# A gated cross-attention kernel on one core: the order of its first stage rewritten, with the next batch's correlation products placed right behind the picking and the context transformed two batches ahead

## What is computed

```python
x = x + tanh(g_xattn[0]) * autocorrelation(layernorm(x), ctx, ctx)
x = x + tanh(g_ffn[0])   * routed_lora_ffn(layernorm(x))
x = x + tanh(g_xattn[1]) * cross_attention(layernorm(x), ctx)
x = x + tanh(g_ffn[1])   * lora_ffn(layernorm(x))
```

```python
corr = ifft(fft(q) * conj(fft(k))).real        # per channel, over 128 lags
w, idx = top_k(corr, 9)                        # 9 = int(2 * ln 128)
w = softmax(w)
out = sum_i w_i * v[min(idx_i + pos, L - 1)]
```

## Time and profile before

| | us |
|---|---|
| median of 3 runs (815.9 to 818.12) | 816.29 |
| the profiled execution | 813.65 |
| its span in the trace | 811.9 |
| PE busy | 774.1 (95%) |
| DVE busy | 577.2 (71%) |
| ACT busy | 412.1 (51%) |
| POOL busy | 364.9 (45%) |

### The profile page before, as it was taken

One profiled execution on the slowest core, in us unless ns is written; L12 is line 12 of the kernel. 1 busy time (PEld: TensorE's weight loads), 2 busy tenths in 40 slices (PEclk: granted clock), 3 DMA queues, 4 the chain that ended last, 5 costly groups with the idle time before them and its releaser, 6 DMA issues.

```text
span 811.9 us, 13195 instructions
## 1 busy us (share of the span) xinstructions
PE 774.1 (95%) x4224; PEld 631.9 (78%) x4224; DVE 577.2 (71%) x1283; ACT 412.1 (51%) x1142; POOL 364.9 (45%) x420
## 2 busy tenths in 40 slices
PE   4699999988999999999999999999999999999998
PEld 1355554667888888888888888888888888888776
DVE  3689999756767777676777766677776666677774
ACT  3246664456545555554565546445555545454521
POOL 1356776646334533643353246424533643254532
PEclk9899999999999999999999999999999999999999
DMA  7300003103100300120031003000310101000002
GB/s 284 115 27 27 26 27 98 45 1 103 29 1 1 105 27 2 42 76 14 1 92 27 14 1 105 27 2 1 104 28 1 52 28 53 1 14 1 1 28 77
DMA packets 16979, 34.61 MB, mean 43 GB/s; under 512 B 2320, under 2 KB 2448, under 8 KB 16656
## 3 DMA queue, kind: packets, MB, share of 16 engines
q1 hardware_dynamic: 16912, 33.78, 13.1%
HBM read 31.67 MB, written 2.10 MB: 42 GB/s over the span
## 4 chain that ended last, share of the span: by engine, by line
PE 68%; DVE 17%; POOL 7%; issue 6%; ACT 1%; DMA 1%; SPq 0%; POOLq 0%; DVEq 0%; ACTq 0%
PE pair L825 17%; PE pair L826 17%; PE pair L827 17%; PE pair L924 4%; PE pair L937 3%; PE pair L986 3%; POOL qkr L512 2%; POOL probn L504 2%; PE pair L926 1%; DVE prod L1160 1%; DVE wlag L1186 1%; POOL wo_lo L498 1%; DVE xres L1243 1%; DVE score L1260 1%; DVE rest L1170 1%
## 5 line engine op out<-in xcount | busy, mean ns | idle before, releaser
L504 POOL TENSOR_TENSOR probn<-prob,erec 128x512 f32<-128x512 f32 x64 | 66.9, 1046 | 162.2 <-DVE erec L1275 162.2
L1299 DVE TENSOR_TENSOR qkn<-pair,qkr 128x640 f32<-128x640 f32 x64 | 52.8, 825 | 91.0 <-POOL qkr L512 91.0
L1280 DVE TENSOR_REDUCE qkss<-qksq 128x5 f32<-128x640 f32 x64 | 52.6, 822 | 86.4 <-ACT qksq L698 86.4
L691 ACT ACTIVATE prob<-score,nmax 128x128 f32<-128x128 f32 x256 | 99.6, 393 | 20.4 <-DVE nmax L1262 18.7
L680 ACT ACTIVATE oT_hi<-pair 128x512 fp32r<-128x512 f32 x64 | 38.2, 597 | 136.2 <-PE pair L827 136.2
L825 PE MATMUL pair<-wq_hi,nT_hi 128*128 128x512 f32 x256 | 105.8, 413 | 0.0
L825 PE MATMUL pair<-wo_hi,oT_hi 128*128 128x512 f32 x256 | 100.8, 394 | 2.8 <-issue 2.8
L827 PE MATMUL pair<-wq_hi,nT_lo 128*128 128x512 f32 x256 | 100.4, 392 | 0.0
L826 PE MATMUL pair<-wo_lo,oT_hi 128*128 128x512 f32 x256 | 100.2, 392 | 0.0
L826 PE MATMUL pair<-wq_lo,nT_hi 128*128 128x512 f32 x256 | 100.2, 391 | 0.0
L827 PE MATMUL pair<-wo_hi,oT_lo 128*128 128x512 f32 x256 | 99.6, 389 | 0.0
(11 more groups left out here) (174 smaller groups left out, 1995.9 us busy)
## 6 DMA issues: line engine op xcount, KB each, us to landing
wq_raw<-in_wq SPq DMA_DIRECT2D x32, 256.0 KB, 2.8
wo_raw<-in_wo SPq DMA_DIRECT2D x32, 256.0 KB, 2.9
wkv_raw<-in_wkv SPq DMA_DIRECT2D x8, 512.0 KB, 4.8
ctxn<-in_ctx_n SPq DMA_DIRECT2D x8, 256.0 KB, 2.9
ctxt<-in_ctx_t SPq DMA_DIRECT2D x8, 256.0 KB, 2.6
out<-wkv_raw SPq DMA_DIRECT2D x8, 256.0 KB, 2.0
xres<-in_x SPq DMA_DIRECT2D x1, 1280.0 KB, 11.7
wbase<-in_wbase SPq DMA_DIRECT2D x1, 1024.0 KB, 9.0
```

Source lines behind the costliest of these rows:

```text
L504: pool.tensor_tensor(probn[:], prob[:], erec[:].unsqueeze(2).broadcast_to([P, HG, P]), ALU.mult).then_inc(normed, 1)
L691: t = act.activation(prob[:, h, :], score[:, h, :], ACT.Exp, bias=nmax[:, h:h + 1], accum_out=esum[:, h:h + 1])
L1280: dve.tensor_reduce(qkss[:], qksq[:], AX.X, ALU.add).then_inc(qk_ss, 1)
L1299: dve.tensor_tensor(qkn[:], qk_bank, qkr[:].unsqueeze(2).broadcast_to([P, HG + 1, P]), ALU.mult).then_inc(qk_nat, 1)
```

## The change

Nothing is computed differently; apart from one subtraction cut in two and one transfer cut in two, the instructions are the same and stand in another order.

- **DVE:** `corr_product(b+1)` comes right behind `pick_lags(b)` and no longer behind `out_products(b)`. The statistics of batch b+2 come behind `out_products(b)` (from b = 2 on) and are woven into `route(b-1)`.
- **PE:** the context transforms of slot b are those of batch b+2. `q_transform(b+1)` stands in the middle of `base_products(b-2)`, `turn_lags(b)` before `routed_product(b-2)`, `correlation(b+1)` before the last two context transforms, and parts of `project_kv(0)` and `project_q(0)` move from the tail into slot 6.
- **ACT:** the normalisation of batch b+1 (`nx`) stands at the start of slot b, ahead of `high_turned_ctx(b)` and the exponentials; the copies of the context are those of b+2 and come after the normalisations; the weights are split one slot earlier.
- **POOL:** `add_bias(b-2)` moves behind `lag_weights(b)`, `sums(b)` before `f_scale(b+2)`, the weights' low parts move one slot earlier (slots 3, 4 and 5 in place of 4, 5 and 6), and `low_wkv` is two operations of 128x512 in place of one of 128x1024.
- **SP:** `dft` comes in two pieces, the first three matrices ahead of the first context; the gates come later. In the tail `squares`, `high_v`, `inverse_norms`, `copy_rows` and their like change places with neighbours.

```diff
                 load_batches(0)
+                sp.dma_start(dft[:, 0:V_IM + 1, :], dft_d[:, 0:V_IM + 1, :]).then_inc(ld_dft[0], 16)
                 load_ctx(0)
-                sp.dma_start(dft[:], dft_d[:]).then_inc(ld_dft, 16)
-                sp.dma_start(gates_in[:], gates[:]).then_inc(ld_g, 16)
+                sp.dma_start(dft[:, V_IM + 1:N_DFT, :], dft_d[:, V_IM + 1:N_DFT, :]).then_inc(ld_dft[1], 16)
                 load_batches(1)
                 load_ctx(1)
+                sp.dma_start(gates_in[:], gates[:]).then_inc(ld_g, 16)
...
-                def low_wkv(g):
+                def low_wkv(g, halves=(0, 1)):
...
                 def a_slot(b):
-                    if has(b - 2):
-                        add_bias(b - 2)
                     low_turned_ctx(b)
                     if has(b - 3):
                         low_rows(b - 3)
-                    if b == 4:
+                    if b == 3:
                         low_wkv(0)
-                    if b in (5, 6):
+                    if b in (4, 5):
...
                     lag_weights(b)
+                    if has(b - 2):
+                        add_bias(b - 2)
...
+                    sums(b)
                     if has(b + 2):
                         f_scale(b + 2)
-                    sums(b)
...
                     if has(b - 2):
                         copy_hw(b - 2)
+                    if b >= 1:
+                        act.wait_ge(q_fwd, b + 1)
+                        normalise(nx[:], b + 1, f_sc, f_root, f_norm)
                     high_turned_ctx(b)
                     lag_exponents(b)
...
                     if has(b - 1):
                         inverse(b - 1)
                     if has(b - 2):
-                        base_products(b - 2)
+                        base_products(b - 2, (0, 1))
+                    q_transform(b + 1)
...
+                    if has(b - 2):
+                        base_products(b - 2, (2, 3))
+                    turn_lags(b)
+                    if has(b - 2):
                         routed_product(b - 2)
-                    q_transform(b + 1)
-                    turn_lags(b)
-                    ctx_transform(b + 1, 0)
                     lag_transforms(b)
...
                     pick_lags(b)
+                    corr_product(b + 1, 0)
+                    corr_product(b + 1, 1)
                     if has(b - 1):
                         add_lagged(b - 1)
...
                     out_products(b)
-                    corr_product(b + 1, 0)
-                    corr_product(b + 1, 1)
+                    if b >= 2 and has(b + 2):
+                        f_first(b + 2)
```

139 lines of the change are left out of this document (88 added, 51 removed).

## The result

The changed kernel takes 821.8 us (median of 4 executions, 820.25 to 823.07) against 816.7 for the kernel before beside it (4 executions, 815.9 to 818.12). The ratio is 1.0067, with a 95% interval from 1.0049 to 1.0084: **slower by 0.7%**, outside the range of 811.6 to 818.8. The profiled execution took 823.07, with a span of 821.3.

The account below looks back on a forecast made before the run. PE, busy 95% of the span, was taken to bound the kernel, with changes possible only before about 140 us. Terms -4.4 - 0.4 + 4.0 + 1.5 - 0.4 - 1.5 = -1.2 took 816.29 to 815.1, range 811.6 to 818.8.

Parts of the forecast that it names:

- What bounds it: Whole kernel: PE is full from about 140 us, so the change gains or loses only before that, moving scores(0).
- Start, -4.4: Up to slot 2: earlier first picking makes slot 2 begin at 46.6 against 51.05; -4.4 us, from -5.5 to -3.4.
- Slot 2, -0.4: Slot 2: no extra POOL or ACT work yet, 15.7 us against 16.09; -0.4.
- Slots 3 to 5, +4.0 and +1.5: Slots 3 to 5: POOL's later run delays lag_weights, slots of 18.4, +4.0; shared access of DVE and POOL, +1.5.
- The port term: Slots 3 to 5: wlag products held by queued POOL operations; 0.5 us a slot, +1.5 in all, from 0 to +3.3.
- upper end: Slots 3 to 5: wlag waits for one POOL operation each, lag_weights ends at 9.3, n1 at 13.3; +1.1 a slot.
- POOL's run before, "it cost PE nothing in itself": Kernel before: POOL's run was over at 107.11, 1.1 us ahead of lag_weights, so it cost PE nothing.
- The rival of the clock (0.12): Before turn_lags, slots 3 to 5: PE's 2.3 us wait lowers the clock, +3 a slot, 824 in all three; chance 0.12.
- Slot 6 and the tail, -0.4 and -1.5: Slot 6 without weights on POOL, 17.0 against 17.44, -0.4; tail with 2.1 us less PE work, -1.5.
- The second stage, taken as unchanged: Behind scores(0): the 64 slots keep their order and were taken at their old length; 0.
- The rule of the Trainium skill: Slots 3 to 5: exclusive port lock makes POOL wait too, 0.9 a slot, +2.7 instead of +1.5, a time of 816.3.

Follow-up runs that it names:

- filled kernel: The changed kernel with PE's waits at the begin of the second stage filled by unread products, the run of experiment 10; 819.8 us.
- filled pair: The kernel before and the changed kernel, both with unread products filling PE's waits at the begin of the second stage; 815.48 and 819.8 us.
- Experiment 1: The changed kernel with POOL's low parts of the weights moved from ahead of lag_weights to the end of the slot; 812.45 us.
- kernel 4: The changed kernel with DVE's correlation products behind add_lagged(b-1) from slot 1 on, the run of experiment 4; 818.73 us.
- experiment 3: The changed kernel with ACT making high_turned_ctx(b+1) ahead of high_rows at the end of slot b; 811.75 us.
- experiment 5: Kernel 4 with two unread products on PE ahead of turn_lags of batches 3 to 5; 820.81 us.
- experiment 14: Experiment 5's kernel with PE's waits at the begin of the second stage also filled by unread products; 816.02 us.
- experiment 15: The changed kernel with unread products filling PE's waits both before turn_lags of batches 3 to 5 and at the second stage's begin; 819.0 us.
- experiment 10: The changed kernel with two unread products on PE in each wait before turn_qk(2) and turn_qk(3) at the second stage's begin; 819.8 us.
- experiment 13: Kernel 4 with PE's waits at the begin of the second stage filled by unread products; 818.94 us.
- experiment 4: The changed kernel with DVE's correlation products behind add_lagged(b-1) from slot 1 on; 818.73 us.
- experiment 2: The changed kernel with routed_product(b-2) ahead of turn_lags(b) on PE again; 823.36 us.
- experiment 9: The kernel before with two unread products on PE in each wait before turn_qk(2) and turn_qk(3) at the second stage's begin; 815.48 us.
- experiment 7: The kernel before with POOL's order of the change alone, and the weights' high parts on ACT one slot earlier; 827.67 us.
- experiment 8: The changed kernel with weights' parts at POOL's slot end, nx and turned context ahead of high_rows, correlation products behind add_lagged; 809.89 us.

## Why the prediction was wrong

The forecast was -1.2. Between the two traces lie +9.4, 10.6 more: 4.4 in slots 3 to 5, 3.2 behind scores(0), 1.9 at the start and 1.1 in the rest. Between the medians lie +5.1.

- **What bounds it.** Right for PE's work: it was decided before scores(0), and slots 3 to 5 decided it.
- **Start, -4.4.** The first picking came at 14.59 (14.7 predicted), the second at 27.50 (28.0). From there slot 1 was too short in the prediction: slot 2 began at 48.59, and at 48.22 in the filled kernel, not at 46.6 (45.5 to 47.7). Behind the second picking it lasts 21.1 and 20.2, where I had 18.6, and the two lag transforms in it ran at the lower clock (2.07 and 1.92, 2.08 and 1.78). The gain of -2.5 in the traces lies outside -5.5 to -3.4. The filled pair's -4.7 agrees with the prediction by luck, as its kernel before began late (first picking at 17.67, slot 2 at 52.88). Experiment 1, which has the same code up to slot 3, did begin slot 2 at 46.63, but because its second picking came at 26.39, with no fall in slot 0; its slot 1 was as long (20.2). So the term holds only within what single executions differ by, and that is as much as half of it.
- **Slot 2, -0.4.** +0.1: PE waited 0.34 for `n1`, and I had allowed 0.2; PE's own work in it came to 15.9, and I had added it up to 15.5.
- **Slots 3 to 5, +4.0 and +1.5.** This is the step that failed. The exponentials ended 4.2 behind `turn_hw` (4.0) and the waits are where I put them. POOL's run ended at 8.1 and not at 7.85 (my terms ahead of POOL add up to 2.65, I went on with 2.85, and `cT_lo` started at 3.0). But `lag_weights` ended at 9.8 and not at 8.95, PE waited 2.7 and not 2.3, and PE's transposes of `n1` started 13.7 behind `turn_hw` and not 12.3. Two terms were too small. The port term: I took 0.5 a slot between 0 and 1.1, and it is the upper end and more (`lag_weights` at 9.8, against 9.3 there): three of four wlag products wait, one behind each POOL operation, so that DVE and no longer POOL's run ends last. Behind it: after `lag_weights` the chain runs over the correlation products, the sum and the statistics on DVE, for which POOL's `h_mv` waits 0.53 even behind the bias. My 13.3 for the upper end fell 0.4 short. Together 1.6 a slot more than 18.4 (20.04 with the clock up), +4.9 in three where I had +1.5; the clock's one fall adds 0.9. Experiments 1 and 3 show that the run in this place costs some 2 us a slot. How that splits between the run's late end and the held products is read from the trace; no run has the one without the other.
- **POOL's run before, "it cost PE nothing in itself".** This reading was wrong, and the trace of before shows it. Slot 3 has no weights on POOL there: no wlag product waits, PE doesn't wait for `lag_weights`, 16.44 us. Slots 4 to 6 have them: one product waits 1.26 to 1.42 in each, PE waits 1.07 to 1.22, 17.30 to 17.44 us. By this comparison the weights cost 0.9 to 1.0 a slot before, and 2.2 in the changed kernel (20.04 less 17.87). DVE and PE, slots 3 and 4 of before:

```profile
72.10 0.29 DVE L1186 SCALAR_TENSOR_TENSOR wlag<-rest,elag 128x128 f32<-128x128 f32 x1
...
88.55 1.26 DVE L1186 SCALAR_TENSOR_TENSOR wlag<-rest,elag 128x128 f32<-128x128 f32 x1
```

```profile
74.42 0.66 PE L873 MATMUL pair<-dft,wlagn 128*128 128x128 f32 x4
...
83.58 0.33 PE L852 MATMUL pair<-dft,hw 128*128 128x128 f32 x1 [0.52 <-DVE hw L1234]
...
91.84 0.66 PE L873 MATMUL pair<-dft,wlagn 128*128 128x128 f32 x4 [1.07 <-POOL wlagn L470]
```

- **The rival of the clock (0.12).** Its mechanism was right, its price too high. The clock fell in one of three slots in each of two traces of the changed kernel, at 0.9 each (20.94 less 20.05), and not 3, since the slower products run partly inside the later wait for `n1`. In kernel 4, without that wait, a fall costs 1.3.
- **Slot 6 and the tail, -0.4 and -1.5.** -0.1 and -1.2.
- **The second stage, taken as unchanged.** Its work is, its clock isn't: the two traces lie 3.2 us apart there, and without the falls all lie within 0.2. The trace of before was an execution without falls in it, 2.6 below its median; that of after had two and lies 1.3 above its own. I carried that gap over as a constant, which the medians bear out only roughly: 5.1 between them, 4.3 in the filled pair.
- **The rule of the Trainium skill** ("SBUF — State Buffer", section "SBUF: two separate sides"), that the two engines exclude each other for a whole instruction, is borne out by the trace for DVE: a wlag product takes 1.35 to 1.38 instead of 0.28. By my estimate it would have made the term 2.7 by POOL's waits for DVE, and these are small: two `wq_lo` operations take 2.65 instead of 2.54 with products queued between them. DVE pays nearly all. The term came out above that estimate, at 4.9, by another path: DVE's own waits and the chain behind them.

## What to carry to other kernels

Before work is moved on GpSimd, look at which VectorE operations with both operands in SBUF fall into its run: here each waited for one GpSimd operation, the run of four held three of them and the run of two held one; a small copy (`ninth`) was held too. A run that cost 0.9 us a slot where it stood cost 2.2 when another engine's new order made it begin 2 us later. When an operation is made earlier, look at the engine that consumes it: the correlation products came 7 us before PE wanted them and only pushed back the chain that PE did wait for.

## What the runs showed of the hardware

- **DVE beside a busy POOL.** wlag, whose operands both lie in SBUF, is held (1.35 instead of 0.28), as is the copy `ninth` in the kernel before (0.89 instead of 0.17). `match_replace` (0.28, beside POOL's subtraction of the weights in slot 4 of before) and the residual sum with one operand in PSUM (0.74, beside POOL's bias) are not. When POOL had operations queued, one DVE operation got in between two of them.
- **The granted clock behind waits.** Waits of PE of 0.5 to 1.2 us before `turn_lags` in slots 3 to 5 had no fall behind them (2 slots of the kernel before, 6 of experiments 1 and 3, and 9 of experiments 5, 14 and 15, where the unread products fill the rest). Waits of 2.65 to 2.71 had one in 1 of 3 slots (after, and experiment 10), 2 of 3 (experiment 13) or 3 of 3 (experiment 4), and waits of 1.83 to 1.85 in 3 of 3 (experiment 2). The same program falls in one execution and not in another; what decides it was not found.
- **The start.** Between single executions the first picking moved by 2.0 us in kernels with the old start (16.93 before, 17.67 in experiment 9, 18.97 in experiment 7) and by 1.8 in kernels with the changed start (14.34 in experiment 3, 14.59 after, 16.16 in experiment 8), where it waits for `bb` to land.
